# Two Mamba branches and a binarized convolution block on one core: a new table of orders for the five engines

## What is computed

```python
def _mamba(x, ...):                     # x: 128 sequences of 32 tokens of 128
    xc, z = split(x @ W_in.T)
    xc = silu(causal_conv4(xc) + conv_b)
    dbc = xc @ W_x.T                    # 8 of rank, 16 of B, 16 of C
    dt = softplus(dbc[..., :8] @ W_dt.T + b_dt)
    h = exp(dt * A) * h + (dt * xc) * B         # a scan over tokens, per state
    y = sum_over_states(h * C) + xc * D_skip
    return (y * silu(z)) @ W_out.T
y1 = _mamba(x.reshape(b * h, w, c), ...1)
y2 = _mamba(x.reshape(b * w, h, c), ...2)
x = y1 + y2 + x
out = conv3x3(relu(batch_norm(x)), sign(w0) * mean|w0|)
out = conv3x3(relu(batch_norm(out)), sign(w1) * mean|w1|)
return out + x
```

## Time and profile before

| | |
|---|---|
| runs shown | 984.59, 982.1, 983.23 us, median 983.23 |
| profiled execution | 987.21 us, of which the span from first to last instruction is 985.4 |
| PE / DVE / ACT / POOL busy | 822.0 / 805.3 / 791.0 / 744.7 us |
| mean granted TensorE clock | 0.910 |
| scans of DVE (L792) | 256, each about 2.28 us |
| POOL products (L526, L517) | 159 + 128, each 2.36 us |
| table loads of ACT inside the items | L629 x15, L593 x15, L634 x15, L635 x16, 1283 ns each |
| DMA | 111.00 MB, mean 113 GB/s |

### The profile page before, as it was taken

One profiled execution on the slowest core, in us unless ns is written; L12 is line 12 of the kernel. 1 busy time (PEld: TensorE's weight loads), 2 busy tenths in 40 slices (PEclk: granted clock), 3 DMA queues, 4 the chain that ended last, 5 costly groups with the idle time before them and its releaser, 6 DMA issues.

```text
span 985.4 us, 13514 instructions
## 1 busy us (share of the span) xinstructions
PE 822.0 (83%) x4614; PEld 388.1 (39%) x4614; DVE 805.3 (82%) x536; ACT 791.0 (80%) x1383; POOL 744.7 (76%) x347
## 2 busy tenths in 40 slices
PE   6777879797988898888898988787989886879898
PEld 3424334242435352424253524242434333434343
DVE  2289989898989898989898989899898989975261
ACT  2699899998989898989898989999998988632130
POOL 0378879898989898989898998989898989810000
PEclk9788888998989898989898989899999988889999
DMA  6706152534343433344251606161515152000001
GB/s 171 259 3 214 44 181 79 170 111 151 109 142 105 145 107 129 131 122 159 72 188 50 209 26 221 60 209 48 195 66 196 64 194 87 1 1 1 1 33 54
DMA packets 39149, 111.00 MB, mean 113 GB/s; under 512 B 7244, under 2 KB 9384, under 8 KB 39080
## 3 DMA queue, kind: packets, MB, share of 16 engines
q1 hardware_dynamic: 36896, 109.81, 33.2%
q10 hardware_dynamic: 2184, 0.33, 0.2%
HBM read 106.97 MB, written 3.15 MB: 112 GB/s over the span
## 4 chain that ended last, share of the span: by engine, by line
PE 29%; issue 22%; DVE 19%; ACT 15%; POOL 14%; POOLq 0%; DMA 0%; ACTq 0%; DVEq 0%
DVE state L792 11%; PE bank L1162 10%; POOL state L526 7%; PE bank L1013 6%; POOL state L517 6%; DVE bank L792 6%; PE bank L1050 5%; ACT bank L593 3%; ACT product L617 2%; ACT L634 2%; PE bank L1006 2%; PE bank L992 2%; PE bank L1058 1%; POOL u L544 1%; PE bank L948 1%
## 5 line engine op out<-in xcount | busy, mean ns | idle before, releaser
L526 POOL TENSOR_TENSOR state<-state,c_wide 128x1024 f32<-128x1024 f32 x159 | 371.8, 2360 | 14.8 <-DVE state L792 14.8
L517 POOL TENSOR_TENSOR state<-u,b_wide 128x1024 f32<-128x1024 f32 x128 | 300.3, 2364 | 65.0 <-PE bank L1013 63.9
L1013 PE MATMUL bank<-state,ident 64*64 64x512 f32 x2048 | 251.3, 611 | 9.7 <-POOL state L526 9.6
L792 DVE TENSOR_TENSOR_SCAN state<-bank,state 128x1024 f32<-128x1024 f32 x96 | 217.8, 2276 | 2.1 <-ACT bank L593 1.8
L617 ACT ACTIVATE product<-u_tok,b_tok 128x256 f32<-128x256 f32 x512 | 213.9, 494 | 0.6
L1006 PE MATMUL bank<-ident,product 128*128 128x128 f32 x1024 | 152.1, 297 | 63.6 <-DVE state L792 43.3
L604 ACT ACTIVATE state<-dt,a_neg 128x512 f32<-128x512 f32 x256 | 166.8, 711 | 19.4 <-PE bank L1013 19.4
L1006 PEld LDWEIGHTS bank<-ident,product 128*128 128x128 f32 x1024 | 125.4, 153 | 134.9 <-issue 75.2
L593 ACT ACTIVATE bank<-dt,a_neg 128x512 f32<-128x512 f32 x256 | 165.0, 675 | 16.6 <-DVE state L792 8.6
L792 DVE TENSOR_TENSOR_SCAN bank<-state,bank 128x1024 f32<-128x1024 f32 x65 | 148.3, 2282 | 5.6 <-PE bank L1006 5.4
L792 DVE TENSOR_TENSOR_SCAN state<-state,bank 128x1024 f32<-128x1024 f32 x63 | 141.7, 2268 | 0.3 <-PE bank L1006 0.3
(11 more groups left out here) (98 smaller groups left out, 688.2 us busy)
## 6 DMA issues: line engine op xcount, KB each, us to landing
c_wide<-bc_rows SPq DMA_DIRECT2D x128, 512.0 KB, 4.7
b_wide<-bc_rows SPq DMA_DIRECT2D x48, 512.0 KB, 6.0
b_wide<-bc_rows SPq DMA_DIRECT2D x32, 256.0 KB, 4.1
x_t<-in_x_dram SPq DMA_DIRECT2D x4, 512.0 KB, 4.8
out_dram<-x_t SPq DMA_DIRECT2D x8, 256.0 KB, 2.0
k_room<-in_L_conv_w_dram SPq DMA_DIRECT2D x2, 576.0 KB, 7.2
bc_rows<-dbc SPq DMA_DIRECT2D x16, 64.0 KB, 1.6
state<-in_L_conv_W_in_dram SPq DMA_DIRECT2D x2, 256.0 KB
```

What stands on the lines that cost most here:

```text
L517: pool.tensor_tensor(tile(n), u[:, :, :], over_halves(b_wide[:, PLAIN.index(s), :]), ALU.mult).then_inc(plain_input, 1)
L526: pool.tensor_tensor(tile(n), tile(n), over_halves(c_wide[:, n % NST, :]), ALU.mult).then_inc(output_pool, 1)
L792: dve.tensor_tensor_scan(flat(target), flat(decay), flat(source), 0.0, ALU.mult, ALU.add).then_inc(scanned, 1)
L1013: return pe.matmul(y_sum[64 * h:64 * h + 64, b, :], weights[rows, :], source[rows, h, :], start=first, stop=last)
```

## The change

It replaces the tables. Numbers of work stay: 8 turned and 8 plain states, 10 outputs on POOL and 6 on DVE per item, the same matmuls. What changes is which states are turned, who multiplies which by C, and in which slot each thing is issued. `SLOTS` (8) and `PRODUCTS` (3) are the same numbers in both. B is loaded in six transfers per item in place of five.

```diff
-TURNED = (2, 5, 8, 10, 12, 13, 14, 15)
+TURNED = (2, 3, 5, 9, 11, 12, 14, 15)
-POOL_C = (1, 3, 4, 6, 9, 10, 11, 12, 14, 15)
+POOL_C = (1, 2, 5, 8, 9, 11, 12, 13, 14, 15)
-B_GROUPS = ((0, 1), (3, 4), (6, 7), (9,), (11,))
+B_GROUPS = ((0, 1), (4,), (6, 7), (8,), (10,), (13,))
...
-PE_TAPS = {15: ((2, 0), (2, 1), (2, 2), (2, 3)), 0: ((1, 4), (1, 5)), 1: ((1, 6), (1, 7))}
-PE_OUT = {10: (0, 1), 12: (2,), 14: (3,)}
-PE_TURNS = {0: (2,), 3: (5,), 6: (8,), 9: (10,), 11: (12,), 12: (13,), 13: (14,), 14: (15,)}
-PE_SUMS = {1: (-3, -2, -1), 3: (0,), 6: (1,), 7: (2, 3), 8: (4, 5, 6), 9: (7,), 10: (8,), 13: (9, 10), 15: (11, 12)}
-POOL_B = {0: (4,), 2: (6, 7), 7: (9,), 9: (11,), 13: (16, 17, 19)}
-ACT_DECAYS = {0: (1,), 1: (3,), 2: (4,), 4: (6,), 5: (7,), 7: (9,), 8: (11,), 15: (16,)}
-ACT_TURNED = {1: (5,), 5: (8,), 7: (10,), 10: (12, 13), 11: (14,), 13: (15, 18)}
-ACT_EARLY = {0: (2,), 1: (8, 10), 8: (12,), 9: (13,), 11: (14,), 12: (15,)}
-ACT_PRODUCTS = {0: (5,)}
+PE_TAPS = {12: ((2, 0),), 13: ((2, 1),), 15: ((2, 2), (2, 3), (2, 4)), 1: ((1, 5),), 2: ((1, 6), (1, 7))}
+PE_OUT = {9: (0, 1), 10: (2, 3)}
+PE_TURNS = {1: (2,), 2: (3,), 4: (5,), 8: (9,), 10: (11,), 11: (12,), 13: (14,), 14: (15,)}
+PE_SUMS = {0: (-4, -3), 2: (-2, -1), 5: (0,), 6: (1, 2, 3), 7: (4,), 8: (5,), 9: (6, 7), 10: (8,), 12: (9, 10),
+           14: (11,)}
+POOL_B = {0: (4,), 1: (6,), 5: (7,), 6: (8, 10), 8: (13,), 12: (16,), 13: (17,)}
+ACT_DECAYS = {0: (1,), 3: (4,), 5: (6,), 6: (7,), 7: (8,), 8: (10,), 12: (13,), 14: (16,)}
+ACT_TURNED = {1: (3, 5), 7: (9,), 10: (11, 12, 14), 13: (15, 18)}
+ACT_EARLY = {0: (2,), 2: (5,), 4: (9,), 8: (11,), 12: (14,)}
+ACT_PRODUCTS = {0: (3,), 9: (12,), 12: (15,)}
 PE_Z = 3
-PE_DBC = 3
-PE_DT = 5
-PE_B_TOK = 11
-PE_U_TOK = (12, 14)
-ACT_XC = 2
+PE_DBC = 4
+PE_DT = 6
+PE_B_TOK = 10
+PE_U_TOK = (13, 15)
+ACT_XC = 3
 ACT_GATE = 4
-ACT_DBC = 4
-ACT_DT = 5
-ACT_EXP = 5
+ACT_DBC = 5
+ACT_DT = 6
+ACT_EXP = 6
 ACT_LN = 7
-ACT_B_TOK = 10
-ACT_U_TOK = (12, 15)
-POOL_REST = 8
+ACT_B_TOK = 11
+ACT_U_TOK = (13, 15)
+POOL_REST = 6
 POOL_U = 10
...
-DVE_POST = 5
-DVE_LOST = 8
-DVE_ADD = 9
-DVE_OUT = 15
+DVE_POST = 3
+DVE_LOST = 7
+DVE_ADD = 8
+DVE_OUT = 11
-POST_INSIDE = False
-LOST_INSIDE = True
-ADD_INSIDE = False
-AT_KERNELS = (11, 12, 13)
+POST_INSIDE = True
+LOST_INSIDE = False
+ADD_INSIDE = True
+AT_KERNELS = (9, 10, 11)
...
-AT_EARLY_OUT = (6, 7, 9, 10)
-AT_EARLY_ADD = (8, 11)
+AT_EARLY_OUT = (4, 5, 7, 8)
+AT_EARLY_ADD = (6, 9)
```

More of the change, by code:

```diff
@@ L467, in _ @@
                 spread_b(k, 1)
+                spread_c(k, 0)
                 spread_b(k, 2)
-                spread_c(k, 0)
                 spread_c(k, 1)
                 spread_b(k, 3)
+                spread_b(k, 4)
                 spread_c(k, 2)
-                spread_b(k, 4)
+                spread_b(k, 5)
                 spread_c(k, 3)
```

## The result

The changed kernel takes 927.66 us (median of 4 runs, 925.88 to 928.72) against 983.05 for the kernel before beside it (982.1 to 984.59): a ratio of 0.9433, with a 95% interval of 0.9412 to 0.9455. The profiled execution takes 925.88 us, its span is 924.1 (before 985.4), and the mean granted clock is 0.961 (before 0.910).

A forecast was written before the change was run, and what follows sets the result against it. No engine full; one chain (gate, dbc projection, dbc copy, decay) halts every item. An item of 46.8 + 0.3 + 0.3 + 0.25 = 47.65 against 51.14 saves 48.9 over 14 periods, with the first item 52: 931 us, range 922 to 955.

The forecast's parts named there:

- the forecast's own bounds: Whole kernel: 922 us if all waits go (47.1 an item), 946 with PE's slow clock (48.65 an item).
- The wait for the rest: DVE's addition, with only scan 8 between it and the lost part, waits 0.3 us per item for POOL's rest.
- the 0.3 on average for outputs: DVE per item: 0.3 us on average for the outputs to add, which six items have.
- 0.25 for handovers: Per item: 0.25 us added for handovers a layout doesn't see, half of DVE's 0.48 lost at the lost part before.
- The layout by hand: One item laid out from its first scan at t = 0, engine by engine, to see whether DVE still waits.
- its thinnest margin: On PE, state 2 is turned by 4.9 behind sum 13; scan 2 wants it at 5.7: margin 0.8 us.
- That alone is off the path.: ACT: two of four table loads go, 2.6 us of 47.3 busy, claimed not to shorten the path by itself.
- The gap of 3.28 is gone by this: DVE's wait before scan 7: decay 7 ready at 19.6, 2.2 us before its scan, decay 6 ahead of the dbc copy.
- A second wait of 1.5 an item: Rival, chance 0.25: a ring through all engines, from sum 13 to POOL's output 13, limits; 49.1 an item, 953 us.
- ACT held longer by a switch: Rival, chance 0.04: each remaining table switch holds ACT 1.28 us more, ACT becomes the bound; 49.3 an item, 955 us.
- The wait only moving: Rival, chance 0.03: the later xc block delays the gate by 3.3 us, the lost part waits instead; 51 an item.
- PE as the bound at the lower clock: Rival, chance 0.04: PE gets the lower clock for a share of its work; at 0.4, 53.9 an item, 1022 us.

The follow-up runs named there:

- the experiment with the lost part: Changed kernel with the lost part set between scan 7 and its multiply instead of behind the multiply: 945.71 us, ratio 0.9631.
- the experiment with the order alone: Kernel before with the decay of state 7 ahead of the dbc copy, nothing else moved, four table loads kept: 985.27 us, ratio 1.0025.

## Why the prediction was right, and where its reasons were not

**The size.** 931 was forecast and 927.66 measured, inside the forecast's own bounds of 922 to 946. By terms: the first item 3 and measured 2.6; the 14 periods 48.9 and measured 56.5; the last item 0 and measured -0.4; the start was not in the sum and gave 2.57. That the median came within 3.3 us is in part luck. The sum put the profiled span at 933, and it is 924.1, 9 less. But the sum took the median to lie 4 below the profiled execution, as it did before, and after the change it lies 1.8 above: 5.8 of the 9 are cancelled by that.

**The period was 47.11, not 47.65.** Its terms can be read. DVE's own work is 46.70 - 0.35 = 46.35, where I took 46.8, the old gaps taken off. DVE's busy time fell by the same 0.45 (46.28 in the earlier trace rows to 45.83) with the same operations: a scan of 2.28 is followed 2.20 behind its start where nothing is waited for the earlier trace rows, one ahead of a gap has no such overlap, and some short pauses without a releaser in the trace are in the old figure too. The wait for the rest is 0.35 (0.3). The six items with outputs take 47.3 to 47.65 and six of the eight others 46.7 to 46.75, so the 0.3 on average for outputs was right. The other two (47.45 and 47.64) lose 0.65 and 0.85 before scan 12, whose turned input comes late: 0.12 on average, where the prediction had 0.25 for handovers. So the 0.45 of DVE and half of the handovers make up the miss.

**What was foreseen as it came.** 31 loads in the items; dbc at 1.91 with no idle before it; POOL's wait for the lost part a small one (0.66 where shown below); DVE's wait for decays gone. The layout by hand held: dbc, put at 14.4 behind scan 0, started at 14.46, dt (18.1) at 18.18 and |v| (19.6) at 19.54. So did its thinnest margin: it did not bind in the changed kernel, and bound when a multiply came 1.14 later and PE's clock fell behind it.

```profile
362.01 2.37 POOL L539 TENSOR_TENSOR sp_l<-dt,sp_l 128x1024 f32<-128x1024 f32 x1 [0.66 <-DVE sp_l L813]
```

**The step that failed: "That alone is off the path."** The loads were costed as ACT's busy time, 2.6 us that nobody waits for, and the gain was put down to the order of decay and copy ("The gap of 3.28 is gone by this"). The runs turn this round. The order by itself gives nothing in the kernel before (985.27) and 4.3 us in the changed one; the loads back in their place take 49.7. Between xc and gate they delay the gate, and PE waits for it ahead of dbc, since dbc is projected into the bank that the gate reads; PE idles 2.65 to 3.58, and dbc takes up to 3.64 in place of 1.91, though not in every item; copy, decay and dt follow late. The hand layout contained this, since it starts dbc at 14.4 behind a gate without loads before it. The number came out right because the layout was, while the sentence that named its cause was not. The 3.28 was the whole chain's delay, seen at the first scan that needed it.

**The rivals.** A second wait of 1.5 an item did not appear in the changed kernel; in the experiment with the lost part a leg of its ring closed. ACT held longer by a switch: the load at 397.02 is followed by a decay at 398.34, and two loads in a row start 1.28 apart with the next work 1.30 behind, so no hold is seen; the drain of about 1.38 us that the Trainium skill (ScalarE: Activation LUTs, What ACT_TABLE_LOAD costs) states for each switch doesn't show in any row here, and the measurement decides. The wait only moving happened, but in the experiment with the order alone. PE as the bound at the lower clock did not happen: the mean granted clock is 0.96, in the item shown and over the span.

## What to carry to other kernels

Price an instruction by its place: the same two table loads cost 3 us an item between two steps of the longest chain and 0.7 elsewhere, against 2.6 of busy time. Of the 3, some 1 us was PE's lower granted clock behind the wait. Where an engine waits for one late thing, follow back what made that late before moving it; putting it ahead of its neighbour in the queue sends the wait to the next in line, and the sum stays the same. Once the long wait is gone, lay out the ring through all engines and find its smallest margin: here the same edit cost 18 us with one sum queued behind the late multiply, and gained 6.4 with that sum moved ahead of it.

## What the runs showed of the hardware

**TensorE after idling.** The four dbc matmuls took 1.91 us after an idle of 0, 0.42 and 1.41 us, and 3.64 after 3.57, where the granted clock in the stretch was 0.50, the level of 1.2 GHz. The length of the idle alone doesn't settle it: in the first item of the changed kernel they took 2.23 with no idle before them. In the changed kernel with the two loads put back the idle was 2.65 in 14 items, and the same four matmuls took 3.5, 3.0, 2.5 or 1.91; the granted clock was 0.63 from 375.70 to 378.70, around the one that took 2.95, and 1.00 from 275.80 to 277.80, around one of 1.91. The fall can also come later than the first work behind a wait: in the changed kernel PE idled 3.30 before 414.74 and turned a state at a granted clock of 1.00 (413.00 to 415.70), and from 416.00 to 418.30 it was 0.52.

**A tiny operation that takes 1.4 us.** The changed kernel within the first item, DVE's timeline and then POOL's:

```profile
89.90 0.15 DVE L777 TENSOR_SCALAR k_mean<-bank 128x2 f32<-128x2 f32 x1
90.08 1.41 DVE L780 TENSOR_TENSOR k_mean_sq<-k_mean 128x2 f32<-128x2 f32 x1
```

```profile
89.11 2.36 POOL L528 TENSOR_TENSOR state<-state,c_wide 128x1024 f32<-128x1024 f32 x1 [2.34 <-DVE state L794]
```

Both of DVE's operations have two columns; the first takes its input from a PSUM bank. The second ends at 91.49, and POOL's multiply, begun before it, at 91.47. In the kernel before it took 1.79 and ended at 101.06, as the second of two multiplies of POOL ended at 101.05. The Trainium skill (SBUF — State Buffer, SBUF: two separate sides) says that a DVE operation with two inputs in SBUF and a GpSimd one that reads SBUF hold a shared pair of ports one at a time, whoever begins first. The rows would agree; no run here tests it.
